# Routing two mixture-of-experts layers by slot tables in one pass, with rows gathered and scattered by token

## The reference, cut to what matters

```
x = x + gated_scan(_layernorm(x)) 
# experts 0: 64 experts, the two best of each token, softmax weights
weights, selected = top_k(layernorm(x) @ gate_kernel, 2); weights = softmax(weights)
h0, h1 = ragged_dot(sorted_x, w0), ragged_dot(sorted_x, w1)     # 256 -> 512, rows sorted by expert
out = ragged_dot(silu(h0) * h1, wo)                             # 512 -> 256
x = x + sum over the two of weights * out
x = x + mamba(_layernorm(x))
# experts 1: 16 experts, the best of each token, its input times sigmoid(logit), and a shared expert
x = x + shared(layernorm(x)) + expert_out
```

## Time and profile before

| | |
|---|---|
| median of 3 runs | 3584.77 us (3583.7 to 3586.59) |
| the profiled execution's own time | 3579.32 us |
| its span, first to last instruction | 3577.6 us |
| busy share of the span | PE 73%, weight loads 50%, DVE 58%, ACT 29%, POOL 32% |
| mean granted TensorE clock | 0.847 of full |

### The profile page before, as it was taken

How to read it: one execution, slowest core, us unless ns; L and a number is a source line. 1 busy time by engine, 2 the same in 40 slices (tenths; PEclk the granted TensorE clock), 3 DMA queues, 4 the chain that set the end, 5 groups by cost and what they waited for, 6 DMA issues and landing times. The chain is left out here.

```text
span 3577.6 us, 38762 instructions
## 1 busy us (share of the span) xinstructions
PE 2609.9 (73%) x11942; PEld 1788.9 (50%) x11942; DVE 2090.5 (58%) x3937; ACT 1044.5 (29%) x1613; POOL 1161.0 (32%) x641
## 2 busy tenths in 40 slices
PE   5555399670599999994276877867777668956993
PEld 2222166460599999993022332333323325636993
DVE  8999767463111212113698998998989963231222
ACT  4444122110111111111345545555455322101110
POOL 0000134305100000004658768677686740021003
PEclk8777699855799999997588888888889888978996
DMA  4110100002799999995200000000100100007995
GB/s 161 64 64 33 40 12 18 13 0 72 239 333 331 332 334 333 333 331 161 65 24 35 25 34 25 24 35 24 36 24 36 36 18 0 0 33 258 332 332 172
DMA packets 299023, 426.74 MB, mean 119 GB/s; under 512 B 23728, under 2 KB 197168, under 8 KB 294848
## 3 DMA queue, kind: packets, MB, share of 16 engines
q1 hardware_dynamic: 264384, 377.58, 31.7%
q0 software_dynamic: 9216, 25.18, 2.3%
q10 hardware_dynamic: 25344, 23.08, 1.9%
HBM read 362.58 MB, written 63.18 MB: 119 GB/s over the span
## 5 line engine op out<-in xcount | busy, mean ns | idle before, releaser
L1275 POOL TENSOR_TENSOR ss_h<-ss_h,ss_cs 128x2048 f32<-128x2048 f32 x128 | 578.8, 4523 | 89.3 <-DVE ss_h L1601 81.4
L1345 PE MATMUL ss_y<-ss_h,all_ident 128*128 128x512 f32 x1024 | 535.2, 672 | 27.9 <-POOL ss_h L1275 27.8
L1060 DVE TENSOR_TENSOR experts_in<-experts_sil,experts_pU 128x512 f32<-128x512 f32 x176 | 121.1, 688 | 665.6 <-PE experts_pU L997 665.6
L1601 DVE TENSOR_TENSOR_SCAN ss_h<-ss_da,ss_c_h,ss_dbu 128x512 f32<-128x512 f32 x384 | 470.7, 1268 | 46.6 <-ACT ss_da L1471 40.6
L1345 PEld LDWEIGHTS ss_y<-ss_h,all_ident 128*128 128x128 f32 x1024 | 222.3, 220 | 315.5 <-issue 279.3
L1471 ACT ACTIVATE ss_da<-ss_dt,ss_decay 128x512 f32<-128x512 f32 x512 | 326.6, 711 | 177.9 <-POOL ss_dt L1251 90.4
L997 PE MATMUL experts_pG<-experts_xt,experts_wg 128*128 128x128 f32 x2816 | 346.5, 277 | 0.0
L997 PE MATMUL experts_pU<-experts_xt,experts_wu 128*128 128x128 f32 x2816 | 343.4, 275 | 0.0
L1006 PE MATMUL experts_pY<-experts_wd,experts_in 128*128 128x256 f32 x1408 | 332.7, 379 | 0.0
L997 PEld LDWEIGHTS experts_pG<-experts_xt,experts_wg 128*128 128x128 f32 x2816 | 331.8, 193 | 0.1
L1594 DVE TENSOR_TENSOR ss_dbu<-ss_dtx,ss_bB 128x1024 f32<-128x1024 f32 x256 | 314.4, 1228 | 28.5 <-PE ss_bB L1337 1.2
(11 more groups left out here) (298 smaller groups left out, 3794.8 us busy)
## 6 DMA issues: line engine op xcount, KB each, us to landing
experts_wg<-in_w SPq DMA_DIRECT2D x128, 512.0 KB, 4.3
experts_wu<-in_w SPq DMA_DIRECT2D x128, 512.0 KB, 5.5
experts_wd<-in_wo SPq DMA_DIRECT2D x128, 512.0 KB, 6.5
ss_cs<-ss_c_rows SPq DMA_DIRECT2D x32, 1024.0 KB, 4.7
experts_wg<-in_gate_up SPq DMA_DIRECT2D x48, 512.0 KB, 4.7
experts_wu<-in_gate_up SPq DMA_DIRECT2D x48, 512.0 KB, 5.9
experts_wd<-in_down SPq DMA_DIRECT2D x48, 512.0 KB, 7.3
experts_xr<-moe_xs SPq DMA_DIRECT2D x176, 128.0 KB, 3.7
```

Of the source, the lines that this page charges most:

```text
L1060: nc.vector.tensor_tensor(IN[t.two][:].rearrange("p f t -> p (f t)"), SIL[t.two][:], pU[t.two][:], ALU.mult)\
L1275: pool.tensor_tensor(h[:], h[:], CS[q % 2][:, n % GROUP].unsqueeze(1).to_broadcast([P, CI, BT]), ALU.mult)\
L1345: mm = pe.matmul(y[:, c], ident[:], H[n % RING][:, c], start=(n == 0), stop=(n == N - 1))
L1601: ins = V.tensor_tensor_scan(H[n % RING][:, c], DA[n % 2][:, c], DBU[:, c % 2], first, ALU.mult, ALU.add)
```

## The change

The rows are no longer sorted in memory. Each expert owns a table in DRAM with room for all 4096 tokens (`lists`, 32 lines of 128 entries for each expert, an entry being the pair of token number and output row). So a token's slot is its expert times 4096 plus its rank, and is known inside the first pass: DVE computes it in `place`, and POOL writes the pair there with an indirect DMA of 128 entries of 8 bytes, while the pass goes on. The second pass is gone. The normalised rows are stored in token order, block by block, from SP (`rows`). After the last block, one indirect DMA reads the table lines that are in use, one for each tile, and PE turns them, so that each tile has a column of tokens and one of output rows (`token`, `place`).

In `expert_tiles` POOL gathers each tile's rows by token, six tiles ahead into eight buffers, and scatters each result to the output row; an empty entry points at a row of zeros (row 4096) and at an output row beyond the bounds, which is skipped. The SP queue keeps the weights alone and ACT's stores are gone. In the second layer the stored row is 512 wide: the input already times its weight (the `weigh` step, four DVE multiplications in each block of the pass), and X with the shared expert added; `copy_y` adds the latter (`direct`) and the scatter writes to `out` itself. `combine` is gone.

In `state_space` the results of experts 0 lie in token order, so SP loads them by eight plain DMAs of 1 MB, into eight buffers (the rings `H`, `CS` and `DA`). DVE's opening is written in another order, statistics come after one block and then for seven, the first block's four parts use the four banks of `y` in place of `Q`, and the last part of the first step sizes moves from POOL to DVE (`first_steps`). In the loop `exp_log` is cut in two, and its exponential is issued one state earlier, before the decays of the next state.

The zero filling in `gate_loop` becomes four DMAs of 3.3 MB together that write the empty entries and the zero rows, and DVE waits for them once, since their source lies in a buffer (`T3`) that DVE writes later.

```
-                fill(0)
-                with sp.Fori(1, NB) as i:
-                    sp.wait_ge(s["xn_done"], i * TPB)
-                    fill(i)
-                sp.wait_ge(s["zeroed"], 16 * NB * len(to_zero))
+                sp.wait_ge(s["consts"], 3 + len(routes))
+                for r, empty in zip(routes, blank):
+                    lists = r.lists.rearrange("(a p) w -> p a w", p=P)
+                    sp.dma_start(lists, empty.rearrange("p s w -> p (s w)").unsqueeze(1).to_broadcast(list(lists.shape)))\
+                        .then_inc(s["zeroed"], 16)
+                    sp.dma_start(r.rows[T:T + P].rearrange("p (a d) -> p a d", d=D),
+                                 zeros[:].unsqueeze(1).to_broadcast([P, r.width // D, D])).then_inc(s["zeroed"], 16)
+                sp.wait_ge(s["zeroed"], 32 * len(routes))
...
+                dve.wait_ge(s["zeroed"], 32 * len(routes))
...
+        self.lists = nc.dram_tensor(f"{tag}_lists", (experts * self.room + P, 2 * P), I32).ap()
+        self.rows = nc.dram_tensor(f"{tag}_rows", (T + P, width), F32).ap()
+        self.ys = out if self.direct else nc.dram_tensor(f"{tag}_ys", (T * k, D), F32).ap()
...
+                rows = r.rows[0:T].rearrange("(b t p) w -> b p t w", p=P, t=TPB)
+                for b in range(NB):
+                    sp.wait_ge(s["xw_done" if shared else "xn_done"], (b + 1) * TPB)
+                    sp.dma_start(rows[b, :, :, 0:D], XN[b % 2][:]).then_inc(rows_stored[b % 2], 16)
+                    if shared:
+                        sp.wait_ge(s["shared_added"], b + 2)
+                        sp.dma_start(rows[b, :, :, D:2 * D], X[:, b * TPB:(b + 1) * TPB]).then_inc(s["x_stored"], 16)
...
-                with pool.Fori(0, NB // 2) as i:
...
-                        for j in range(TPB):
-                            for k in range(K):
-                                pool.indirect_dma_start(r.xs, bass.IndirectOffsetOnAxis(ap=SL[h][:, j, k:k + 1], axis=0),
-                                                        XS[h][:, j], None).then_inc(sent[h], 16)
...
+                for b in range(NB):
+                    pool.wait_ge(s["slots_ready"], b + 1)
+                    for j in range(TPB):
+                        for k in range(K):
+                            pool.indirect_dma_start(lists, bass.IndirectOffsetOnAxis(ap=SL[b % 2][:, j, k:k + 1], axis=0),
+                                                    entry[:, b * TPB + j, k], None).then_inc(listed[b % 2], 16)
                 for h in range(2):
-                    pool.wait_ge(sent[h], SENT * (NB // 2))
+                    pool.wait_ge(listed[h], LISTED * (NB // 2))
+                pool.wait_ge(s["list_done"], 1)
+                pool.indirect_dma_start(LST[:].rearrange("p s w -> p (s w)"), None, r.lists,
+                                        bass.IndirectOffsetOnAxis(ap=LIST_I[:], axis=0)).then_inc(r.fetched, 16)
...
+                    V.scalar_tensor_tensor(SL[b % 2][:], IDX[:], float(T), RK[:], ALU.mult, ALU.add).then_inc(s["slots_ready"], 1)
...
+                        if b < NB - 2:
+                            normalise(b + 2)
...
+                ch.mark(V.scalar_tensor_tensor(JUNKS[1], END[:], part[:], FREE[:], ALU.is_le, ALU.mult, accum_out=LIST[:]))
...
+                V.tensor_tensor(LIST_I[:], LIST[:], part[:], ALU.add).then_inc(s["list_done"], 1)
...
-                def send(i, again):
...
-                        if again:
-                            dve.wait_ge(sent[h], i * SENT)
...
-                        ch.link(V.tensor_tensor(at(r.slot), BASE[:], at(RKA), ALU.add))
-                        V.tensor_tensor(SL[h][:], BASE[:], at(RKA), ALU.add).then_inc(s["rows_ready"], 1)
...
+                def gather(t):
+                    if t >= TURN:
+                        pool.wait_ge(s["xt_raw"], t - TURN + 1)
+                        pool.wait_ge(s["y_done"], t - TURN + 1)
+                    pool.indirect_dma_start(XR[t % TURN][:], None, r.rows, bass.IndirectOffsetOnAxis(ap=r.token[:, t:t + 1], axis=0))\
+                        .then_inc(x_loaded[t % TURN], 16)
+                def scatter(t):
+                    pool.wait_ge(s["y_done"], t + 1)
+                    to = bass.IndirectOffsetOnAxis(ap=r.place[:, t:t + 1], axis=0)
+                    pool.indirect_dma_start(r.ys, to, Y[t % BUF][:], None, bounds_check=T * r.K - 1, oob_is_err=False)\
+                        .then_inc(stored[t % BUF], 16)
+                for t in range(AHEAD):
+                    gather(t)
+                for t in range(N):
+                    if t + AHEAD < N:
+                        gather(t + AHEAD)
+                    scatter(t)
...
+                    if r.direct:
+                        nc.vector.tensor_tensor(Y[t.w][:], XR[t.b][:, D:2 * D], pY[t.two][:, 0:D], ALU.add).then_inc(s["y_done"], 1)
+                    else:
+                        nc.vector.tensor_scalar(Y[t.w][:], pY[t.two][:, 0:D], 1.0, None, ALU.mult).then_inc(s["y_done"], 1)
...
-def combine(nc, tag, X, r, out=None):
...
+                fetch(0)
...
+                for b in range(1, NB):
+                    fetch(b)
...
-                    project(Q[:], WI, c * P, HT[b % 2], KD).then_inc(s["x_raw"], 1)
+                    project(bank(b, c), WI, c * P, HT[b % 2], KD).then_inc(s["x_raw"], 1)
...
+                def first_steps():
+                    ch = Chain(dve, s["tail"])
+                    for half in range(2):
+                        part = slice(2 * half, 2 * half + 2)
+                        e, u = DTX[0][:, part], DT[0][:, part]
+                        wait(dve, "exp_done", 1)
+                        ch.link(V.tensor_scalar(REST, e, 1.0, 1.0, ALU.add, ALU.subtract))
+                        ch.link(V.tensor_tensor(REST, e, REST, ALU.subtract))
+                        ch.link(V.tensor_tensor(u, u, REST, ALU.add))
+                    for half in range(2):
+                        part = slice(2 * half, 2 * half + 2)
+                        u = DT[0][:, part]
+                        wait(dve, "ln_done", 1)
+                        V.tensor_tensor(u, u, LN1[:, part], ALU.add).then_inc(s["dt_done"], 1)
+                        wait(dve, "dt_done", half + 1)
+                        V.tensor_tensor(DTX[0][:, part], u, XC[0][:, part], ALU.mult).then_inc(s["dtx_done"], 1)
...
+                dve.wait_ge(s["loaded"], LOADED)
+                dve.wait_ge(s["decay_done"], 1)
+                V.tensor_scalar(DECAY[:], DECAY[:], -1.0, None, ALU.mult).then_inc(s["decay_done"], 1)
                 add_experts(1)
+                add_experts(2)
                 for c in range(CI):
                     convolve(0, c)
-                add_experts(2)
+                    add_experts(c + 3)
+                add_experts(NB - 1)
                 split_bc(0)
-                add_experts(3)
-                row_stats(1, NB // 2 - 1)
+                row_stats(1, NB - 1)
+                first_steps()
```

## The result

| | before | after |
|---|---|---|
| median | 3584.56 us, 4 runs (3583.7 to 3586.59) | 3380.2 us, 4 runs (3375.62 to 3385.05) |
| the profiled execution's own time | 3579.32 us | 3385.05 us |
| its span | 3577.6 us | 3383.3 us |

The ratio is 0.9429 with a 95% interval of 0.9413 to 0.9446: 204 us less. Forecast were 3363 us and a range of 3340 to 3398. The forecast made its sum against the profiled execution before, so its span after should have been 3577.6 - 222 = 3355.6 us; it was 3383.3, 27.7 more.

The account below looks back on a forecast made before the run. PE was taken to bound the expert stages, DVE the mamba loop, POOL's indirect DMAs the stretches between. Terms -81 - 46 + 3 - 46 + 0 - 54 + 2 = -222 gave 3363 us from the median 3584.8; range 3340 to 3398.

Parts of the forecast that it names:

- the four gains: First route stage -81 us, second route stage -46, opening of `state_space` -46, the end after the last expert tile -54.
- first route stage: last slots: First route pass: DVE gets the last ranks at 813.9; reading ranks, count and slots take 2.2 us, giving 816.1.
- The pass over the blocks keeps its period: First route stage: the period stays 10.71 us, with POOL's 8 scatters of 10.1 us a block hidden behind it.
- The rival with a POOL price of 1.52 us: First route pass: POOL becomes the bound, 12.2 us a block for 10.7, +12 and +2: 3378 us, chance 0.13.
- The tails of the expert stages: Program's end: last result at 3517.7, scatter 1.3, landing 2.9, exit 1.4, so 3523.3 against 3577.6: -54 us.
- Six gathers beside the first weights: Start of both expert stages: six POOL gathers compete with the first weights PE waits for, +1 and +2 us.
- The period of 5.52: Expert stages: PE stays the bound and a tile still takes 5.52 us; as a rival, chance 0.58, 3363 us.
- 348 GB/s fits: Second layer's expert stage: 1.922 MB a tile is 348 GB/s, which fits since the engines moved 374 GB/s.
- The gather is 33 us ahead: Expert stages: each tile's gather is issued 33 us ahead, so POOL's 2.5 us of work in 5.52 fits.
- The opening of `state_space`: Mamba stage's start: first scan at about 93 us instead of 139, -46 us, with the eight loads hidden.
- the exponential's move: Mamba loop: delays one set of decays by 1.9 us where the boundary waits for POOL anyway: 0, else +4.
- The gate loop's +2: Gate loop: the fills' 3.3 MB follow 5.8 MB of loads, so DVE waits for them: +2 us (0 to +5).

Follow-up runs that it names:

- the series of four: The kernel after, but in the first layer four of each block's eight scatters are sent in the pass, the others behind it: 3393.6 us (0.9475).
- the series of six: The kernel after, but in the first layer six of each block's eight scatters are sent in the pass, sixteen more behind it: 3380.6 us (0.9442).
- the POOL that computes: Kernel with all scatters held behind the pass, plus eight unused POOL additions of 128x512 in each block of the first layer's pass: 3499.3 us, one run.

## Why the forecast was right, and where it was off

The mechanism was right, and so were three of the four gains, each within 10 us. The first route stage gave 65.6 us instead of 81. The total lay inside the range although every large miss went the same way. By stage, in us of the profiled executions:

| stage | forecast | measured | off by |
|---|---|---|---|
| gate loop | +2 | 0 | -2 |
| first route stage: last slots | 816.1 | 835.5 | +19.4 |
| from there to experts 0 | 24.9 | 21.2 | -3.7 |
| experts 0 | 723.6 + 1 | 732.4 | +7.8 |
| mamba opening to the first scan | 93 | 94.0 | +1 |
| its loop | 0 | +1.2 | +1.2 |
| second route stage | -46 | -49.3 | -3.3 |
| experts 1 and end | -54 + 2 | -44.3 | +7.7 |

These come to +28.1, against 27.7 of the spans.

**"The pass over the blocks keeps its period"** is the step that failed, on the chip of the profile. The rival with a POOL price of 1.52 us named the right stage and about the right size (+14) for the wrong reason: POOL's scatters took 0.96 + 0.30 us as taken (one here and there up to 1.20), and in the pass POOL waited for DVE, not DVE for POOL. Results of PE that came late in a long series of indirect DMAs, or just behind it, reached DVE and ACT 1.1 to 10.2 us late. Series of four do not do this, a pause of 1.2 us between fours all but removes it, and neither the written-out code nor the row stores play a part. The first chip showed the scatters as the cause and the series of four; the second showed the pauses, the series of six and the POOL that computes; both had a run with the eight scatters and the late signals, as in the first profile after. What in a series of DMAs delays a signal is not shown.

A third chip shows none of it, with the pass at 10.5 us, the last slots at 813.8 and a span of 3358.8. The 3.2 us to the forecast's 3355.6 are luck in part. The expert stages took 9.1 and 7.0 us longer there than forecast, the route stages 5.9 and 6.1 us less, and the kernel before is faster there too, so that the gain was 215 us and not 222. What distinguishes the chips, or the occasions, is open, and so is whether gathers would do the same; no run told these apart.

**The tails of the expert stages** were mis-sized. Forecast were +1 for all of experts 0 and 5.6 us from the last result (3517.7 to 3523.3) to the end. Measured from the end of the last result to the next stage: 9.3 us instead of 4.2 in the first layer, and 12.3 to the program's end. The larger part of what is missing is POOL's drain of 4.87 and 7.90 us. For the route stages the forecast took the time to leave from a stage that ended with POOL's DMAs (6 us) and came out right; for the expert stages it did not carry it over, though they end with POOL's DMAs too since the change. The drain of 7.79 us at the end of the kernel before was hidden behind adds and a store. Why it is 4.87 us in one stage and 7.90 in the other is open.

**The starts.** Six gathers beside the first weights were priced at +1 and +2; the first result of experts 0 comes 25.3 us into the stage instead of 21.5 (882.07 from 856.75), +3.9, and in experts 1 +0.9.

**The period of 5.52** held: 128 results in 697.4 us against 697.6 before. In experts 1 48 results took 258.6 against 256.2. "348 GB/s fits" was right by a hair. "The gather is 33 us ahead" was wrong, and harmless: the gather of a tile in the middle of experts 0 is issued at 1122.29 and the tile is turned at 1141.61, 19.3 us later, and so for all its neighbours. Half of the tiles ahead would have turned the gain into a loss.

**The opening of `state_space`** went as worked out. In the timeline after:

```profile
1595.19 1.67 DVE L1498 SCALAR_TENSOR_TENSOR all_x<-ss_h,moe_weight,all_x 128x256 f32<-128x256 f32 x4 [3.72 <-DMA ss_h<-moe_ys]
...
1613.69 8.91 PE L1252 MATMUL ss_y<-ss_ht,ss_wi 128*128 128x512 f32 x16 [0.78 <-ACT ss_ht L1390]
...
1618.90 1.55 DVE L1549 SCALAR_TENSOR_TENSOR ss_y<-ss_xr,ss_conv_w,ss_y 128x512 f32<-128x512 f32 x2 [4.89 <-ACT ss_y L1397]
```

The first projection stands 24.5 us into the stage (24.1 forecast), the first convolution 29.7 (29.3), the last one ends at 48.3 (48.7). The loads were no part of it. That the exponential's move costs nothing was right within 1.2 us.

**The gate loop's +2** came (DVE's squares start at 28.21 instead of 26.19, waiting 1.72 us for the fill) but was given back before the next stage: the first ranks stand at 734.54, before at 734.59.

## What to carry to other kernels

When a wait moves from one engine's results to a queue in order, count the lead from the last thing that the queue must pass before, in steps of the consumer: three tiles ahead was one. When POOL's indirect DMAs become the last work of a stage, price POOL's drain (here 5 to 8 us) with them, and let another engine wait for their landing, which then passes beside the drain (1.4 us in each stage here). And before a stretch of POOL's DMAs is laid over a tight ring of other engines, look in the old trace for waits that no instruction explains beside such DMAs; if there are any, the overlap may cost a good part of what it saves, and on which chip one measures decides.

## What was not expected of the hardware

- Beside eight back-to-back indirect DMAs of POOL (10 us), results of PE that came 6.7 us or more into the series, or up to 2 us behind it, were taken up 1.1 to 10.2 us late, on two chips of three. With four in a row none was more than 0.4 us late. It cost 22 us in a pass of eight blocks of 10.5 us.
- POOL's drain at the end of a stage of indirect DMAs takes 4.87 and 7.90 us, also when POOL comes to it sooner; where POOL had nothing to do it took 0.03. ACT's after its plain stores took 0.01.
- A POOL that adds 128x512 tiles stretched DVE's steps on 128x64 from 0.18 and 0.22 us in the mean to 0.55 and 0.58, by holding every second one until its addition was over, while its DMA issues left them alone.
- The first route pass, written out for eight blocks, took 2.7 us less from the first ranks to the last than as a hardware loop of the same instructions.
